# Second self attention: heads outside and batches inside, the next head projected beside attention, values in three split passes, division at the sum into x

## The chip, the cores and the metric

The kernel runs on one core of one Trainium2 chip. The metric is the device time of one execution, in microseconds (us), as the median of several runs; lower is better. The engines are TensorE (PE in the profile, with its weight loads as PEld), VectorE (DVE), ScalarE (ACT), GpSimd (POOL) and SyncE (SP), which here only issues DMAs. They run side by side and are held together by semaphores.

## What is computed

The reference is a decoder of two layers over x, 8 batches of 256 tokens with 256 channels. Six stages follow each other, each adding to x what it makes of the layer-normalised x. The change touches the fourth, the self attention of layer 1. Its reference, cut to what matters (HEADS = 8, DIM_HEAD = 128, context of 2 x 512 rows with 192 channels; `_split_heads` joins a head's batches, so that every query meets all 1024 keys):

```python
qh = _split_heads(jnp.einsum('bnq,qi->bni', x, Wq))
kh = _split_heads(jnp.einsum('bmc,ci->bmi', context, Wk))
vh = _split_heads(jnp.einsum('bmc,ci->bmi', context, Wv))
sim = jnp.einsum('hid,hjd->hij', qh, kh) * SCALE
mean = jnp.mean(sim, axis=-1, keepdims=True)
sim = (sim - mean) * ATTN_MATRIX_SCALE + mean
attn = jax.nn.softmax(sim, axis=-1)
out = jnp.einsum('hij,hjd->hid', attn, vh)
...
return jnp.einsum('bni,iq->bnq', out, Wout) + bout
```

So each of 8 heads has 2048 queries (8 batches of 256) and 1024 keys, 128 wide. The softmax doesn't see the subtraction of the mean, and the factor 1.5 goes into the scaling of the queries.

## The kernel before, in words

All arrays have 128 partitions. `x_all` holds x as 16 tiles of 128 tokens; `normalise` (L135) makes `xnT_all`, the normalised x with channels on partitions, for all batches, and issues the loads of the stage's weights on SP's queue. `psum` has 8 banks of 512 fp32 columns.

An fp32 matmul appears in the trace as two records of PE, each with its own weight load. Where more accuracy per pass is wanted, an operand is split: a high part in the faster fp32r format, made by ACT from PSUM, and a low part, the difference, made by DVE. `split_product` (L117) then makes three fp32r matmuls: high by high, low by high, high by low (L121 to L123).

`attention1` (L1366) works in two phases.

Keys and values come first, for all heads at once: 32 parts of 512 columns, 16 of keys and 16 of values. Each is two fp32 matmuls, one over the first 128 context channels and one over the other 64 (L1426 keys, L1429 values), into the eight banks in turn. ACT and DVE take the keys as high and low part (L1489, L1521); of the values one takes one half and the other the other half, as plain fp32 (L1489, L1525).

Then a loop over 8 batches (`Fori`, one body for all). SP copies the batch's slice of `xnT_all` to `xnT` (L1412). PE projects the queries of all 8 heads, fp32, 32 records (L1445); ACT and DVE take them as high and low (L1494, L1535). The attention itself runs over 16 units, a unit being one head and 128 tokens, in the order of `scores_softmax_value_order` (L877): scores of unit u, transposes of unit u-1, values of unit u-2.
- Scores: two halves of 512 keys, three fp32r passes each. DVE takes the negated row maximum (L1541), ACT the exponential with the row sum (L1501).
- Turn: 8 transposes of the 128x1024 weights to key-major form, through banks 4 and 5 (L1466). DVE copies one half out, ACT the other (L1548, L1508).
- Values: 8 fp32 matmuls of 128 columns, the turned weights stationary (L1475). DVE multiplies the result by the inverse of the sum into `o` (L1553, L1555).

When all 16 units of a batch are done, `turn_and_project` (L1334) transposes `o` in 16 transposes (L1341), ACT copies them (L1355), PE makes the output projection in 16 fp32 matmuls, 32 records (L1346), and DVE adds the result to x (L1569), to which it had added the bias at the start of the batch (L1532).

What sets the order: each engine runs its instructions strictly in the order written; there is no planner. PE has unit u's scores ahead of the transposes of u-1, so that the softmax of u runs beside them. The waits on PE at the batch's start are on `x_here`, `out_taken` and `q_taken` (L1436, L1438, L1441, L1452), at its end on `head_taken` (L1478) and the turned output (L1343).

Of the kernel before, what the change touches and what calls it, by code (L numbers as in the profile page):

```python
# [8 lines left out]
F32 = mybir.dt.float32  # L9
I32 = mybir.dt.int32  # L10
F32R = mybir.dt.float32r
# [4 lines left out]
P = 128  # L16
# [1317 lines left out]
def turn_and_project(pe, psum, ident, o, oT, w, turned, turned_taken, out_ready, b, chunks):  # L1334


    for t in range(TT):
        for g in range(chunks // 4):
            for i in range(4):
                lo = (4 * g + i) * P  # L1340
                ins = pe.transpose(psum[:, 2 * t + g, i * P:(i + 1) * P], o[:, t, lo:lo + P], ident[:])  # L1341
            ins.then_inc(turned, 1)
    pe.wait_ge(turned_taken, b * 4 + 4)  # L1343
    for t in range(TT):
        for k in range(chunks):
            ins = pe.matmul(psum[:, 4, t * D:(t + 1) * D], oT[:, t, k, :], w[:, k, :], start=(k == 0),  # L1346
                            stop=(k == chunks - 1))
    ins.then_inc(out_ready, 1)


def take_turned_output(act, psum, oT, turned, turned_taken, b):

    for n in range(4):
        act.wait_ge(turned, b * 4 + n + 1)
        act.activation(oT[:, n // 2, 4 * (n % 2):4 * (n % 2) + 4, :], psum[:, n, :].rearrange("p (k n) -> p k n", n=P),  # L1355
                       ACT.Copy).then_inc(turned_taken, 1)


# [4 lines left out]

def attention1(nc, norm, x_all, xnT_all, ident, psum, a):  # L1366
    with ExitStack() as stack:
# [6 lines left out]
        kT = [s.sb(f"kT_{part}", [P, AH, KEYS], F32R) for part in ("hi", "lo")]  # L1374
        qT = [s.sb(f"qT_{part}", [P, AH, T], F32R) for part in ("hi", "lo")]
        v = s.sb("v", [P, KB, AH * AD])
        xnT = s.sb("xnT", [P, CC, T])
        weights = [s.sb(f"weights{i}", [P, KEYS]) for i in range(2)]
        turned_w = s.sb("turned_w", [P, 2, KEYS])
        U = AH * TT  # L1380
        negmax, sums = s.sb("negmax", [P, U]), s.sb("sums", [P, U])

        o, oT = wk, turned_w[:].rearrange("p t (h d) -> p t h d", h=AH)
        loaded, x_here = s.sem("loaded"), s.sem("x_here")
        kv_ready, kv_act, kv_dve = s.sem("kv_ready"), s.sem("kv_act"), s.sem("kv_dve")
        q_ready, q_high, q_taken, scored, max_ready, exp_done, turned = (
            s.sem(n) for n in ("q_ready", "q_high", "q_taken", "scored", "max_ready", "exp_done", "turned"))
        half_taken = s.sems("half_taken", 2)
        summed, head_taken, own = s.sem("summed"), s.sem("head_taken"), s.sem("own")
        o_turned, o_turned_taken, out_ready, out_taken = (  # L1390
            s.sem(n) for n in ("o_turned", "o_turned_taken", "out_ready", "out_taken"))
        loads = []
        for dst, src in ((ctxT, a["ctxT"]), (wk, a["wk"]), (wv, a["wv"])):
# [4 lines left out]
        HALF = KEYS // 2  # L1398

        parts = [("k", h, half) for h in range(AH) for half in range(2)] + \  # L1400
                [("v", st, half) for st in range(KB) for half in range(2)]

        KP = 2 * AH

        act_did = lambda n: n + 1 if n < KP else KP + (n - KP) // 2 + 1
        dve_did = lambda n: n + 1 if n < KP else KP + (n - KP + 1) // 2

        @block.sync
        def _(sp):
            with sp.Fori(0, B) as b:  # L1410
                sp.wait_ge(q_ready, b * 4)
                sp.dma_start(xnT[:], xnT_all[:, bass.ds(b, 1), :, :]).then_inc(x_here, 16)  # L1412

        @block.tensor
        def _(pe):
            pe.wait_ge(loaded, 16 * len(loads))
            for n, (kind, i, half) in enumerate(parts):
                if n >= 8:

                    if n - 8 < KP or n % 2 == 1:  # L1420
                        pe.wait_ge(kv_dve, dve_did(n - 8))
                    else:
                        pe.wait_ge(kv_act, act_did(n - 8))
                for c, rows in enumerate((P, CTX - P)):
                    if kind == "k":
                        ins = pe.matmul(psum[:, n % 8, :], wk[0:rows, c, i * AD:(i + 1) * AD],  # L1426
                                        ctxT[0:rows, c, half * HALF:(half + 1) * HALF], start=(c == 0), stop=(c == 1))
                    else:
                        ins = pe.matmul(psum[:, n % 8, :], ctxT[0:rows, c, i * P:(i + 1) * P],  # L1429
                                        wv[0:rows, c, half * HALF:(half + 1) * HALF], start=(c == 0), stop=(c == 1))  # L1430
                ins.then_inc(kv_ready, 1)
            pe.wait_ge(kv_act, act_did(len(parts) - 1))
            pe.wait_ge(kv_dve, dve_did(len(parts) - 1))
            with pe.Fori(0, B) as b:
                S0 = b * U
                pe.wait_ge(x_here, b * 16 + 16)  # L1436

                pe.wait_ge(out_taken, b)  # L1438
                for m in range(AH // 2):
                    if m >= 2:  # L1440
                        pe.wait_ge(q_taken, b * 4 + m - 1)  # L1441
                    for j in range(2):
                        for c in range(CC):
                            lo = (2 * m + j) * AD
                            ins = pe.matmul(psum[:, 6 + m % 2, j * T:(j + 1) * T], wq[:, c, lo:lo + AD], xnT[:, c, :],  # L1445
                                            start=(c == 0), stop=(c == CC - 1))
                    ins.then_inc(q_ready, 1)
                for what, k in scores_softmax_value_order(U):
                    h, t = k // TT, k % TT
                    if what == "scores":  # L1450
                        if k == 0:
                            pe.wait_ge(q_taken, b * 4 + 4)  # L1452
                        if k >= 2:
                            pe.wait_ge(exp_done, S0 + k - 1)
                        for half in range(2):
                            ins = split_product(pe, psum[:, 2 * (k % 2) + half, :],
                                                [q[:, h, t * P:(t + 1) * P] for q in qT],
                                                [keys[:, h, half * HALF:(half + 1) * HALF] for keys in kT], True, True)
                        ins.then_inc(scored, 1)
                    elif what == "turn":  # L1460
                        pe.wait_ge(exp_done, S0 + k + 1)
                        for half in range(2):
                            pe.wait_ge(half_taken[half], S0 + k)
                            for j in range(4):
                                lo = half * HALF + j * P
# [3 lines left out]
                    else:  # L1469
                        for half in range(2):  # L1470
                            pe.wait_ge(half_taken[half], S0 + k + 1)
# [700 lines left out]
```

## Time and profile before

| | |
|---|---|
| median of 3 runs | 3400.91 us (3396.31 to 3406.21) |
| the profiled execution: time | 3403.3 us |
| the profiled execution: span of the trace | 3401.4 us |
| mean granted TensorE clock | 0.893 |
| PE busy | 2926.5 us, 86% of the span |
| weight loads (PEld) busy | 2085.1 us, 61% |
| DVE busy | 1863.0 us, 55% |
| ACT busy | 1617.8 us, 48% |
| POOL busy | 685.0 us, 20% |
| DMA | 60.88 MB, mean 18 GB/s |

The span runs from the first to the last instruction on the core; the time has 1.9 us around it. Shares of busy time are means over six stages with different limits; the stage of the change is the stretch from 1745 to 2571 us, between two runs of `normalise`. Matmuls are pipelined: the duration of one record is longer than the distance between the starts of two, and the distance is what PE's time is made of. The granted clock is 1.00 at 2.4 GHz and 0.50 at 1.2 GHz.

### The profile page before, as it was taken

Reading aid. Unit: us, or ns where it says so; the run is one execution under the profiler, and the core shown is the slowest. Engines: PE = TensorE matmul, PEld = TensorE weight load, DVE = VectorE, ACT = ScalarE, POOL = GpSimd, SP = SyncE. Lnnn points to the kernel's source line nnn. Section 1 sums busy time; section 2 is a strip of 40 time slices with the busy share of each in tenths; the row PEclk is TensorE's granted clock in tenths of the full one; section 3 lists DMA queues with packets and bytes.
Section 4 is the critical chain, followed back from the end, with each engine's and each line's share of the span. In section 5 each row is a group of like instructions: output and inputs, shape, how many; then the busy total and the mean of one; then the engine's idle time right before and its main releaser. Section 6 shows DMA issues by size and latency. Waiting matters only on the chain. (4 is left out here: it accounts for less than half of the span.)

```text
span 3401.4 us, 50572 instructions
## 1 busy us (share of the span) xinstructions
PE 2926.5 (86%) x17024; PEld 2085.1 (61%) x17024; DVE 1863.0 (55%) x4064; ACT 1617.8 (48%) x2895; POOL 685.0 (20%) x798
## 2 busy tenths in 40 slices
PE   6788888888655489999979999999998999968998
PEld 3344444444334356776732888888886777747887
DVE  4777877787633456656531444444444544544444
ACT  3887888878721234444511333333333555532221
POOL 1122222222100044444500000000001655620000
PEclk8888988899766689999965999999998999968999
DMA  2000000000010110110110000000002000010000
GB/s 94 4 4 3 3 0 3 3 3 0 1 35 19 54 44 23 23 42 22 21 58 0 4 3 3 3 3 3 3 0 85 4 6 6 3 69 22 6 6 28
DMA packets 88230, 60.88 MB, mean 18 GB/s; under 512 B 54816, under 2 KB 76704, under 8 KB 87648
## 3 DMA queue, kind: packets, MB, share of 16 engines
q1 hardware_dynamic: 88160, 59.99, 5.8%
q8 instruction: 39, 0.64, 0.1%
q14 instruction: 31, 0.25, 0.0%
HBM read 41.10 MB, written 8.39 MB: 15 GB/s over the span
## 5 line engine op out<-in xcount | busy, mean ns | idle before, releaser
L1772 POOL TENSOR_SCALAR x_weights<-x_weights,x_sums 128x256 f32<-128x256 f32 x256 | 231.7, 924 | 1066.5 <-DVE x_sums L1809 1066.5
L670 DVE SCALAR_TENSOR_TENSOR a_w<-a_w,a_sinks 128x384 f32<-128x384 f32 x512 | 332.7, 714 | 31.5 <-ACT a_w L505 31.5
L1074 POOL TENSOR_SCALAR f_weights<-f_weights,f_sums 128x256 f32<-128x256 f32 x256 | 232.2, 924 | 271.2 <-DVE f_sums L1304 271.2
L1501 ACT ACTIVATE a_weights<-psum,a_negmax 128x1024 f32<-128x1024 f32 x128 | 142.5, 1114 | 293.1 <-DVE a_negmax L1541 293.1
L484 ACT ACTIVATE a_e<-psum 128x1024 f32<-128x1024 f32 x192 | 195.4, 1018 | 158.0 <-PE psum L343 118.9
L1475 PE MATMUL psum<-a_v,a_turned_w 128*128 128x128 f32 x2048 | 248.3, 275 | 0.0
L1475 PEld LDWEIGHTS psum<-a_v,a_turned_w 128*128 128x128 f32 x2048 | 238.1, 192 | 0.0
L1541 DVE TENSOR_REDUCE a_negmax<-psum 128x1 f32<-128x1024 f32 x128 | 156.7, 1224 | 124.9 <-PE psum L123 124.0
L1232 ACT ACTIVATE f_weights<-psum,f_negmax 128x256 f32<-128x256 f32 x256 | 117.8, 472 | 215.1 <-DVE f_negmax L1298 215.1
L340 PE MATMUL psum<-a_qT,a_kT_half 32*128 32x512 f32 x512 | 166.5, 730 | 60.6 <-DVE a_w L685 48.7
L685 DVE SCALAR_TENSOR_TENSOR a_w<-a_e,psum 128x512 f32<-128x512 f32 x256 | 162.6, 675 | 96.1 <-ACT a_e L486 86.6
L486 ACT ACTIVATE a_e<-a_e 128x1024 f32<-128x1024 f32 x192 | 202.9, 1057 | 6.1
L1742 ACT ACTIVATE x_weights<-x_masked_s,x_negmax 128x256 f32<-128x256 f32 x256 | 126.9, 496 | 147.1 <-DVE x_negmax L1805 147.0
L505 ACT ACTIVATE a_w<-a_w 128x1536 f32<-128x1536 f32 x128 | 179.4, 1472 | 0.4
L1466 PE MATMUL psum<-all_ident,a_weights 128*128 128x128 f32 x1024 | 133.8, 274 | 9.5 <-ACT a_weights L1501 9.5
L1466 PEld LDWEIGHTS psum<-all_ident,a_weights 128*128 128x128 f32 x1024 | 118.3, 140 | 29.9 <-ACT a_weights L1501 14.2
L370 PE MATMUL psum<-a_w,a_v 128*32 128x512 f32 (+1 forms) x1024 | 114.6, 575 | 19.8 <-DVE a_w L670 19.8
L188 PE MATMUL psum<-all_ident,ln_xn 128*128 128x128 f32 x192 | 53.4, 434 | 82.3 <-DVE ln_xn L177 82.3
L121 PE MATMUL psum<-a_kT_hi,a_qT_hi 128*128 128x512 f32 x256 | 110.7, 432 | 11.3 <-DVE a_qT_lo L1535 11.3
L340 PEld LDWEIGHTS psum<-a_qT,a_kT_half 32*128 32x128 f32 x512 | 44.1, 210 | 113.5 <-DVE a_w L685 59.8
L343 PEld LDWEIGHTS psum<-a_future,a_ident_r 128*128 128x128 f32 x256 | 42.5, 209 | 113.5 <-issue 113.5
L566 POOL TENSOR_TENSOR a_ctxn<-a_ctx,a_vnull 128x256 f32<-128x256 f32 x64 | 45.1, 725 | 330.2 <-DVE a_ctx L640 330.2
(304 smaller groups left out, 6820.1 us busy)
## 6 DMA issues: line engine op xcount, KB each, us to landing
a_xnT<-all_xnT_all SPq DMA_DIRECT2D x16, 256.0 KB, 2.3
x_ctxT<-in_x_ctxT SPq DMA_DIRECT2D x16, 256.0 KB, 2.7
f_xnT<-all_xnT_all SPq DMA_DIRECT2D x16, 256.0 KB, 2.3
f_pv_rows<-f_pv SPq DMA_DIRECT2D x8, 512.0 KB, 3.1
f_pv_groups<-f_pv_rows SPq DMA_DIRECT2D x8, 512.0 KB
f_w<-in_f_w SPq DMA_DIRECT2D x2, 2048.0 KB, 10.3
all_x_all<-in_x SPq DMA_DIRECT2D x1, 2048.0 KB, 8.4
a_wq<-in_a_wq SPq DMA_DIRECT2D x2, 1024.0 KB, 9.2
```

What stands on the lines that cost most here:

```text
L340: pe.matmul(psum[:, 2 * x + h, :], kT_half[rows[h], step % 2, g, 0:P], qT[rows[h], g, 2 * x:2 * x + 2, :], start=True, stop=False)
L484: act.activation(e[:, x, :], psS[x], ACT.Exp).then_inc(exp_done, 1)
L486: act.activation(e[:, x, :], e[:, x, :], ACT.Ln, bias=1.0).then_inc(ln_done, 1)
L505: act.activation(wu, wu, ACT.Silu, scale=SILU_SCALE).then_inc(silu_done, 1)
L670: ins = dve.scalar_tensor_tensor(part, part, sinks[:, col:col + 1], part, ALU.is_ge, ALU.mult)
L685: ins = dve.scalar_tensor_tensor(wu[:, h, 2 * x:2 * x + 2, 0:T], by_branch(e[:, x, :]), CAP, by_branch(psS[x]), ALU.min, ALU.max)
L1074: ins = pool.tensor_scalar(w, w, sums[:, k, h, t:t + 1], None, ALU.mult)
L1466: ins = pe.transpose(psum[:, 4 + half, j * P:(j + 1) * P], weights[k % 2][:, lo:lo + P], ident[:])
L1475: ins = pe.matmul(psum[:, 6 + k % 2, 0:AD], turned_w[:, k % 2, j * P:(j + 1) * P], v[:, j, h * AD:(h + 1) * AD], start=(j == 0), stop=(j = ...
L1501: act.activation(weights[k % 2][:], psum[:, 2 * (k % 2):2 * (k % 2) + 2, :].rearrange("p a n -> p (a n)"), ACT.Exp, bias=negmax[:, k:k + 1 ...
L1541: dve.tensor_reduce(negmax[:, k:k + 1], psum[:, 2 * (k % 2):2 * (k % 2) + 2, :].rearrange("p a n -> p (a n)"), AX.X, ALU.max, negate=True) ...
L1772: ins = pool.tensor_scalar(w, w, sums[:, k, h, t:t + 1], None, ALU.mult)
```

## The change

The order of the loops is turned round: 8 heads outside, 8 batches inside, written out as 64 pairs (head, batch) without a hardware loop. Keys, values and queries are held for two heads only, and all three as high and low part; those of the first head are made in 8 steps ahead of the pairs, and pair n makes one eighth of the keys or values (`project_kv`, a quarter of the keys or two blocks of the values) and one batch's queries (`project_q`) for the next head. Scores and transposes of a unit stay as they were. The turned weights are now split too, by ACT (high) and DVE (low), for all halves of both units of a pair; the value product is 8 blocks of three fp32r passes with the values stationary and 256 tokens moving, so that its result already has channels on partitions. It isn't divided: ACT copies it to `oT`, PE projects it with the head's part of the output weights (two fp32 matmuls of 256 columns), and DVE multiplies by the inverse sums in adding to x, once per pair and head. POOL adds the bias to x at the start. The copies of `xnT_all` on SP, the transposes of `o` and `turn_and_project` are gone. The diff, cut to its core:

```diff
-            with pe.Fori(0, B) as b:
...
-                        for j in range(KB):
-                            ins = pe.matmul(psum[:, 6 + k % 2, 0:AD], turned_w[:, k % 2, j * P:(j + 1) * P],
-                                            v[:, j, h * AD:(h + 1) * AD], start=(j == 0), stop=(j == KB - 1))
...
-                turn_and_project(pe, psum, ident, o, oT, wo, o_turned, o_turned_taken, out_ready, b, AH)
+            def project_kv(n):
+                h, i = n // B, n % B
+                if n >= B:
+                    wait(pe, out_taken, n - B - 1)
+                    wait(pe, kv_low, n)
+                elif n >= 4:
+                    pe.wait_ge(kv_low, n - 3)
+                if n == B:
+                    pe.wait_ge(q_low, B)
+                for j in range(1 if i < 4 else 2):
+                    for c, rows in enumerate((P, CTX - P)):
+                        if i < 4:
+                            ins = pe.matmul(kv_bank(n), wk[0:rows, c, h * AD:(h + 1) * AD],
+                                            ctxT[0:rows, c, i * QUARTER:(i + 1) * QUARTER], start=(c == 0), stop=(c == 1))
+                        else:
+                            lo = (2 * (i - 4) + j) * P
+                            ins = pe.matmul(kv_bank(n)[:, j * AD:(j + 1) * AD], ctxT[0:rows, c, lo:lo + P],
+                                            wv[0:rows, c, h * AD:(h + 1) * AD], start=(c == 0), stop=(c == 1))
+                ins.then_inc(kv_made, 1)
...
+            def turn(u):
+                pe.wait_ge(exp_done, u + 1)
+                for half in range(2):
+                    wait(pe, low_taken, 2 * (u - 1) + half + 1)
...
+            def values(n):
+                h = n // B
+                pe.wait_ge(low_taken, 4 * n + 4)
+                pe.wait_ge(q_low, min(n + 2 + B, A1_PAIRS))
+                wait(pe, oT_ready, n)
+                for j in range(KB):
+                    ins = split_product(pe, psum[:, 6, 0:T], [z[:, h % 2, j, :] for z in v],
+                                        [z[:, n % 2, j, :] for z in turned_w], j == 0, j == KB - 1)
+                ins.then_inc(summed, 1)
+
+            def out(n):
+                h = n // B
+                pe.wait_ge(oT_ready, n + 1)
+                pe.wait_ge(kv_low, min(n + 2 + B, A1_PAIRS))
+                wait(pe, out_taken, n)
+                for t in range(TT):
+                    ins = pe.matmul(psum[:, 7, t * D:(t + 1) * D], oT[:, t * P:(t + 1) * P], wo[:, h, :], start=True, stop=True)
+                ins.then_inc(out_made, 1)
...
+            for n in range(B):
+                project_kv(n)
+                project_q(n)
+            for n in range(A1_PAIRS + 2):
+                here = n < A1_PAIRS
+                if here:
+                    scores(2 * n)
+                if 1 <= n <= A1_PAIRS:
+                    turn(2 * n - 1)
+                if n >= 2:
+                    out(n - 2)
+                if n + B < A1_PAIRS:
+                    project_q(n + B)
+                if here:
+                    scores(2 * n + 1)
+                    turn(2 * n)
+                if 1 <= n <= A1_PAIRS:
+                    values(n - 1)
+                if n + B < A1_PAIRS:
+                    project_kv(n + B)
```

The orders for a pair on ACT (first), the bias on POOL (second), and the order on DVE (third):

```diff
+            for n in range(A1_PAIRS + 1):
+                here = n < A1_PAIRS
+                if n >= 1:
+                    for half in range(2):
+                        high(2 * n - 1, half)
+                if here:
+                    exps(2 * n)
+                if n + B < A1_PAIRS:
+                    q_hi(n + B)
+                if here:
+                    for half in range(2):
+                        high(2 * n, half)
+                    exps(2 * n + 1)
+                if n >= 1:
+                    take_oT(n - 1)
+                if n + B < A1_PAIRS:
+                    kv_hi(n + B)
...
+            for b in range(B):
+                x_b = x_all[:, b * TT:(b + 1) * TT, :]
+                pool.tensor_tensor(x_b, x_b, bo[:].unsqueeze(1).to_broadcast([P, TT, D]), ALU.add).then_inc(x_biased, 1)
...
+            for n in range(A1_PAIRS + 2):
+                here = n < A1_PAIRS
+                if here:
+                    row_max(2 * n)
+                if 1 <= n <= A1_PAIRS:
+                    for half in range(2):
+                        low(2 * n - 1, half)
+                    invert(2 * n - 1)
+                if n >= 2:
+                    add_out(n - 2)
+                if n + B < A1_PAIRS:
+                    q_lo(n + B)
+                if here:
+                    row_max(2 * n + 1)
+                    for half in range(2):
+                        low(2 * n, half)
+                    invert(2 * n)
+                if n + B < A1_PAIRS:
+                    kv_lo(n + B)
```

`high` and `low` are 128x512 from a bank of turned weights, `add_out` is two operations of 128x256, `kv_hi`, `kv_lo`, `q_hi`, `q_lo` and `take_oT` are 128x256.

## Rows read from the trace of the kernel before

**Rows 1.** The page's first line.
```profile
span 3401.4 us, 50572 instructions
```

**Rows 2.** Busy by stretch: us, PE, PEld, DVE, ACT, POOL, PEclk, DMA share, GB/s.
```profile
1745.00:1874.00 129.00, 128.25 (x128) 31.96 (x128) 16.56 (x24) 15.61 (x25) 0.00 (x0) 0.50 0.01 2
1874.00:1878.00 4.00, 3.51 (x8) 2.86 (x9) 0.72 (x2) 0.00 (x0) 0.00 (x0) 0.50 0.01 2
1880.00:1884.00 4.00, 3.83 (x18) 3.00 (x16) 1.39 (x2) 1.33 (x3) 0.00 (x0) 1.00 0.00 0
...
1974.00:2060.00 86.00, 81.16 (x559) 73.06 (x558) 39.79 (x70) 32.91 (x57) 0.00 (x0) 1.00 0.01 3
1745.00:2571.00 826.00, 785.02 (x4608) 622.34 (x4608) 339.00 (x588) 278.51 (x481) 0.00 (x0) 0.92 0.01 3
```

**Rows 3.** Who waited for whom in 1745 to 2571: us in total, times, longest.
```profile
ACT a_weights L1501 <- DVE a_negmax L1541: 293.1, 128, 3.7
...
PE psum L1466 <- ACT a_weights L1501: 9.5, 8, 1.2
```

**Rows 4.** Timeline of one unit: start us, us, engine, line, operation, xcount.
```profile
2001.25 0.48 PE L121 MATMUL psum<-a_kT_hi,a_qT_hi 128*128 128x512 f32 x1
...
2001.57 0.39 PE L122 MATMUL psum<-a_kT_lo,a_qT_hi 128*128 128x512 f32 x1
...
2002.73 1.03 PE L1466 MATMUL psum<-all_ident,a_weights 128*128 128x128 f32 x8
2002.93 1.22 DVE L1541 TENSOR_REDUCE a_negmax<-psum 128x1 f32<-128x1024 f32 x1 [0.97 <-PE psum L123]
...
2003.60 1.95 PE L1475 MATMUL psum<-a_v,a_turned_w 128*128 128x128 f32 x16
...
2004.27 1.11 ACT L1501 ACTIVATE a_weights<-psum,a_negmax 128x1024 f32<-128x1024 f32 x1 [2.36 <-DVE a_negmax L1541]
...
2005.31 0.48 PE L121 MATMUL psum<-a_kT_hi,a_qT_hi 128*128 128x512 f32 x1
```

**Rows 5.** Timeline of the key projection, weight loads of two fp32 matmuls.
```profile
1749.03 0.50 PEld L1426 LDWEIGHTS psum<-a_ctxT,a_wk 128*128 128x128 f32 x2 [1.50 <-issue]
...
1751.03 0.50 PEld L1426 LDWEIGHTS psum<-a_ctxT,a_wk 64*128 64x128 f32 x2 [1.50 <-issue]
```

**Rows 6.** Timeline: output projection and query projection of one batch.
```profile
2041.94 7.17 PE L1346 MATMUL psum<-a_wo,a_turned_w 128*128 128x256 f32 x32 [0.84 <-ACT a_turned_w L1355]
...
2049.99 7.14 PE L1445 MATMUL psum<-a_xnT,a_wq 128*128 128x256 f32 x32 [0.88 <-DVE all_x_all L1569]
```

**Rows 7.** Timeline of the experts' stage: passes of split products, the first and the seventh.
```profile
3077.41 0.28 PE L123 MATMUL psum<-f_xnT_hi,f_w_in_lo 128*128 128x256 f32 x1
...
3078.12 0.28 PE L123 MATMUL psum<-f_xnT_hi,f_w_in_lo 128*128 128x256 f32 x1
```

**Rows 8.** Timeline of the switch attention: 64-row matmuls, transposes, the next group.
```profile
1693.86 1.14 PE L1171 MATMUL psum<-f_kT,f_qT 64*128 64x256 f32 x8
1694.93 1.09 PE L1185 MATMUL psum<-all_ident,f_weights 128*128 128x128 f32 x8
1695.95 1.08 PE L1199 MATMUL psum<-f_turned_w,f_v 128*64 128x256 f32 x8
```

**Rows 9.** Groups of instructions in 1745 to 2571, DVE and ACT.
```profile
L1521 DVE TENSOR_TENSOR a_kT_lo<-psum,a_kT_hi 128x512 fp32r<-128x512 f32 x16 | 11.1, 691 | 56.1 <-ACT a_kT_hi L1489 56.1
...
L1508 ACT ACTIVATE a_turned_w<-psum 128x512 f32<-128x512 f32 x128 | 75.3, 588 | 6.0 <-PE psum L1466 6.0
```

**Rows 10.** Busy time by stretch, first self attention (columns as in rows 2).
```profile
97.00:107.00 10.00, 10.00 (x32) 3.11 (x32) 6.90 (x10) 4.76 (x5) 0.00 (x0) 0.50 0.01 2
...
110.90:117.00 6.10, 6.10 (x30) 2.82 (x26) 4.43 (x8) 5.85 (x5) 0.00 (x0) 1.00 0.00 0
```

**Rows 11.** DMA queues and busy time (columns as in rows 2) of 2614 to 2700.
```profile
q8 instruction: 4, 0.07, 0.3%
...
2614.00:2700.00 86.00, 83.53 (x550) 61.54 (x552) 42.55 (x175) 48.92 (x143) 52.82 (x59) 0.98 0.03 7
```

More of the change, by code:

```diff
@@ L1331, in _ @@
             over_batches(dve, body)
[L1334 to L1356, printed above, removed]
 AH, AD = 8, 128
@@ L1397, in attention1, with kv_bank, q_bank @@
         block = stack.enter_context(nc.Block())
[L1398 to L1412, printed above, removed]
+        def kv_bank(n):
+            return psum[:, 2 * n % 8, 0:T] if n < B else psum[:, 7, 0:T]
+        def q_bank(n):
+            return psum[:, (2 * n + 1) % 8, 0:T] if n < B else psum[:, 6, T:2 * T]
         @block.tensor
@@ L1416, in _ @@
             pe.wait_ge(loaded, 16 * len(loads))
[L1417 to L1431, printed above, removed]
@@ L1481, in part_of @@
-        def part_of(to, n):
-            kind, i, half = parts[n]
-            return to[:, i, half * HALF:(half + 1) * HALF]
+            def project_kv(n):
[17 more added lines that the diff above has]
+                ins.then_inc(kv_made, 1)
@@ new lines, in project_q @@
+            def project_q(n):
+                h, b = n // B, n % B
+                if n >= B:
+                    pe.wait_ge(kv_low, B)
+                    pe.wait_ge(q_low, n)
+                    wait(pe, oT_ready, n - B - 1)
+                elif n >= 4:
+                    pe.wait_ge(q_low, n - 3)
+                for c in range(CC):
+                    ins = pe.matmul(q_bank(n), wq[:, c, h * AD:(h + 1) * AD], xnT_all[:, b, c, :],
+                                    start=(c == 0), stop=(c == CC - 1))
+                ins.then_inc(q_made, 1)
@@ new lines, in turn @@
+            def turn(u):
+                pe.wait_ge(exp_done, u + 1)
+                for half in range(2):
+                    wait(pe, low_taken, 2 * (u - 1) + half + 1)
+                    for j in range(4):
+                        lo = (4 * half + j) * P
+                        ins = pe.transpose(psum[:, 4 + half, j * P:(j + 1) * P], weights[u % 2][:, lo:lo + P], ident[:])
+                    ins.then_inc(turned, 1)
+            def values(n):
[7 more added lines that the diff above has]
+                ins.then_inc(summed, 1)
@@ new lines, in exps, with take_oT @@
+            def exps(u):
+                act.wait_ge(max_ready, u + 1)
+                wait(act, turned, 2 * (u - 1))
+                wait(act, inverted, u - STAT_RING + 1)
+                act.activation(weights[u % 2][:], psum[:, 2 * (u % 2):2 * (u % 2) + 2, :].rearrange("p a n -> p (a n)"),
+                               ACT.Exp, bias=negmax[:, u % STAT_RING:u % STAT_RING + 1],
+                               accum_out=sums[:, u % STAT_RING:u % STAT_RING + 1]).then_inc(exp_done, 1)
+            def take_oT(n):
+                act.wait_ge(summed, n + 1)
+                wait(act, out_made, n)
+                act.activation(oT[:], psum[:, 6, 0:T], ACT.Copy).then_inc(oT_ready, 1)
```

221 lines of the change are left out of this document (90 added, 131 removed).

## Prediction

> **What bounds the kernel now.** I read the page, then busy time by stretch, the stage's waits, and last the timeline of one unit. The profiled execution has a span of 3401.4 us and a time of 3403.3 [rows 1]; the median of the three runs, 3400.9, is 2.4 lower, so the sum is made against 3403.3 and then moved by -2.4. The second self attention lies at 1745 to 2571, 826 us; PE is busy 785 of them, DVE 339, ACT 279 [rows 2]. The reader should see three pieces in it. First, all keys and values are projected in 129 us, in which PE is always busy and the granted clock is 0.50 (1.2 GHz) throughout. Then the clock goes to 1.00 (2.4 GHz) within some 4 us of the query projection. Then come eight batches of 86 us at 1.00 [rows 2].
>
> In a batch PE sets the pace. ACT waits 293 us for DVE's row maximum, but PE waits for the exponentials only 9.5 us in the whole stage, in 8 places [rows 3]: ACT's wait is idle time of an engine that isn't the bound. One unit (head, half of the tokens) shows it: from one first score matmul to the next 2001.25 to 2005.31 = 4.06 us, without a hole on PE. Within it: six score passes, 0.32 for the first and then (2002.73 - 2001.57)/5 = 0.232 each, 1.48 together; eight transposes 0.87 (0.109 each); sixteen records of eight fp32 value matmuls 1.71 (0.107 each) [rows 4]. The first pass after fp32 work costs 0.09 more than the others: call it a change of kind, 0.1. A batch is 16 such units, 65 us; the other 21 are four waits between phases, 7.1 us of query projection and 7.2 of output projection (32 records each, (7.14 - 0.38)/31 = 0.218 per record of 256 columns) [rows 6], and 2 of output transposes.
>
> **The change, part by part.** What counts is PE's time for a pair (head, batch), 64 pairs.
> - Scores, twice: 12 x 0.232 = 2.78. Weight transposes, 16 x 0.109 = 1.74. Both stay.
> - Values: fp32 becomes three fp32r passes, with the value tile stationary and 256 tokens moving: 8 blocks x 3 = 24 passes in place of 32 records. The experts' stage runs just this form, 128x128 against 128x256, fp32r, at (3078.12 - 3077.41)/6 = 0.118 [rows 7]: 24 x 0.118 = 2.83 instead of 3.42. Saves 0.6.
> - Changes of kind: three per pair (two scores, values), 0.3; two before. Bounds 0 and 0.1 each.
> - Output projection per pair: 2 matmuls, 4 records x 0.218 = 0.87, as before. The transposes of the normalised output (0.22 per pair) and the four waits per batch go.
> - Sum without projections: 2.78 + 1.74 + 2.83 + 0.30 + 0.87 = 8.52; x 64 = 545.
> - Queries of the next head, in 56 pairs: 4 records, 0.87. Keys or values of the next head, in 56 pairs: the same columns as before, now in the warm loop. A key part is 4 records of 256 (0.87), a value part 8 of 128 (8 x 0.107 = 0.86).
> - Change of row count: these parts alternate a 128-row and a 64-row chunk. Before, each fp32 matmul took 2.00 us there (loads at 1749.03 and 1751.03) [rows 5], where 1024 columns at 1.2 GHz are 1.71: 0.29 for each change. In the switch attention at full clock, eight transposes that follow 64-row matmuls take 1.02 (1694.93 to 1695.95) [rows 8] against 0.87: 0.15. I take 0.15, since it was measured at the loop's clock and is half of 0.29; ends 0 and 0.29. A key part has two changes, a value part four, mean 3: 0.45. Projections: 0.87 + 0.87 + 0.45 = 2.19; x 56 = 123.
> - Ahead of the loop: first head's keys, values and queries for all batches, 8 steps. At full clock 0.87 + 0.87 and the changes, 17.6 in all; at half clock 4 x (2.29 + 1.74) + 4 x (2.86 + 1.74) = 34.5. Keys and values alone never raised the clock in 129 us, queries did in some 4 us [rows 2], and in the first attention 10 us of full PE work stayed at 0.50 before it rose by 110.9, 14 us after its start [rows 10]. The new stretch is half the one and half the other: I take the rise at 14 us, 14 + 20.5/2 = 24; ends 18 and 35.
> - Start and end: the first query's rest (about 1.2), the first transpose waiting for its exponential (0.4), and behind the last scores the lower half of the weights (0.9), the copy to oT (0.8), the add (1.1): 4.4. Handovers as in rows 4: PE to DVE 0.2, DVE to ACT 0.12.
>
> Sum: 545 + 123 + 24 + 4.4 + 1.2 of stage change = 698, against 826: -128. 3403.3 - 128 = 3275, and with -2.4, **3273**.
>
> **What must stay hidden.** DVE per pair: two maxima 2.44 [rows 4], four lower halves 2.76 [rows 9], and four operations half as wide as those of 0.69, so at most 2.76: 8.0, and two reciprocals of one column. ACT: two exponentials 2.6 with their sums, four copies 2.36 [rows 9], three narrower ones under 1.8: 6.7. Both lie under PE's 10.7, but their queues are in order. The tightest place is the transpose of the even unit: row maximum, then ACT's two upper halves of the odd unit before, then the exponential, done 2.9 us after the scores' end; PE has 0.87 + 0.87 + 0.87 + 1.48 = 4.1 of other work there. Slack 1.2, and 0.3 in the last eight pairs, where there is no projection. Values wait for the query's lower half of the same pair (DVE done near 5.7 of the pair, values due at 6.4). Output waits for the key part's lower half, done 1.3 before it is due. Costed at nothing: eight 256 KB copies and their SP queue (no wait of the stage names them); ACT's eight table loads (ACT waits anyway); the bias on POOL, which starts at once, while the first add comes after two pairs and then one add per 10.7 us (at DVE's 0.69 each, 6 us; uncovered it would cost those 6).
>
> The new stage is written out for 64 pairs, without loops. PE takes some 140 instructions per pair. The cross attention's written-out stretch at 2614 to 2700 fetched 4 instruction blocks in 86 us while PE was hardly stopped [rows 11]; I take zero.
>
> **Against the trace, a rule that speaks against the change.** The experts' rows show loads of the same 128 rows hidden under 256-column passes: 0.118 per pass, hardly above 256 columns at 2.4 GHz [rows 7]. The Trainium skill, TensorE: Matmul & The Clock Gate, section Part 3: Packing small matmuls, says that a weight load overlaps a running matmul only when the row groups differ. By that rule all 24 loads of a pair's values would be exposed; this trace disagrees with it, so the sum goes by the rows. It is the first rival below.
>
> **Rivals.**
> 1. Exposed loads in the values (ends slower). Each pass would carry its load: by half of the K/V matmul's 0.29 [rows 5], 0.15 x 24 x 64 = +223, 3496. It decides from 128/1536 = 0.083 per pass. For: three loads per block where values had two. Against: the same form at 0.118. Chance 0.03.
> 2. The softmax chain stalls PE. If handovers or the order of ACT's queue eat the slack of 1.2 and 1 us more in each pair, +64: 3337. For: slack is only 0.3 in the last eight pairs. Against: the schedule above. Chance 0.10; still faster.
> 3. The cold clock comes along: 64-row parts keep the clock at 0.50 in the prologue and at times in the loop. Prologue +11; each 10 us of loop at half clock +5. With six such dips 3315. Against: batches stayed at 1.00 in spite of their waits. Chance 0.07.
> 4. More gain: no cost for changes of rows (-25) and of kind (-13): 3235. Chance 0.08.
> 5. The change doesn't do what it says for the values: at 0.142 per pass, 24 passes cost the old 3.42. +38, 3311. For: passes that alternate between two kinds of operand tiles; against: the experts' do the same [rows 7]. Chance 0.03.
>
> **How the numbers follow.** The forecast keeps 0.69, its own span 3245 to 3310. Range: from the free changes (3235) to rival 2 less some (3330). Faster by over 0.3% (about 10 us, what this measurement can tell): all but rival 1 and unforeseen stalls, 0.95; within 0.3%, 0.01; slower 0.04, rival 1 and its like.
>
> **What the profile would show.** PE busy without holes, a pair every 10.6 to 10.8 us (8.5 in the last eight); clock 1.00 from the loop's start; value passes 0.118 apart; no 129 us stretch at 0.50; stage near 698 us. Wrong, if PE shows idle before the transposes (waiting for ACT), or value passes 0.2 apart, or a clock of 0.50 within the loop.

## The result, and the profile after

The changed kernel takes **3268.7 us** (median of four runs, 3266.4 to 3270.6), against 3399.3 for the kernel before (four runs): a ratio of 0.961, 95% interval 0.9596 to 0.9624, 130.7 us less. The forecast was 3273, with a range of 3235 to 3330. The profiled execution took 3266.4 us.

The page of the profile after: the span, the engines' busy time, the instruction queue, and the groups of the value passes, of the two parts that the turned weights now have, and of the row maximum.

```profile
span 3264.6 us, 49578 instructions
...
PE 2818.9 (86%) x16640; PEld 2049.9 (63%) x16640; DVE 1942.7 (60%) x4248; ACT 1693.0 (52%) x3120; POOL 694.7 (21%) x806
...
q8 instruction: 68, 1.11, 0.1%
...
L1506 ACT ACTIVATE a_turned_w_hi<-psum 128x512 fp32r<-128x512 f32 x256 | 139.0, 595 | 195.2 <-PE psum L1440 195.1
...
L1570 DVE TENSOR_REDUCE a_negmax<-psum 128x1 f32<-128x1024 f32 x128 | 156.7, 1224 | 89.8 <-PE psum L123 89.8
...
L1577 DVE TENSOR_TENSOR a_turned_w_lo<-psum,a_turned_w_hi 128x512 fp32r<-128x512 f32 x256 | 163.7, 681 | 2.3 <-ACT a_turned_w_hi L1506 2.3
L121 PE MATMUL psum<-a_turned_w_hi,a_v_hi 128*128 128x256 f32 x512 | 150.2, 293 | 0.7 <-DVE a_turned_w_lo L1577 0.7
```

Against [rows 1] the span is 136.8 us shorter. PE has 108 us less to do, DVE 80 more and ACT 75 more, and neither of the two became the bound: the lower halves of the turned weights (681 ns) cost about what the row of the old key halves had promised (691) [rows 9].

Busy time by stretch, with the columns of [rows 2]: the two halves of the part ahead of the pairs, the middle of the pairs, and the whole stage from its first projection to its last add.

```profile
1744.80:1758.90 14.10, 14.09 (x28) 8.02 (x28) 2.55 (x6) 2.30 (x6) 9.81 (x8) 0.50 0.00 0
1758.90:1770.30 11.40, 11.40 (x53) 8.46 (x52) 3.82 (x9) 3.46 (x9) 0.00 (x0) 1.00 0.01 2
1777.50:2390.00 612.50, 605.65 (x3782) 526.30 (x3782) 375.00 (x690) 316.44 (x633) 0.00 (x0) 1.00 0.00 1
1744.80:2441.40 696.60, 686.31 (x4224) 591.73 (x4224) 416.89 (x768) 353.03 (x705) 9.81 (x8) 0.99 0.00 1
```

The stage takes 696.6 us where it took 824.8 (1745.05 to 2569.85), **128.2 less**. The 129 us at a granted clock of 0.50 [rows 2] are gone; 14 us of it are left at the start, and within the pairs the clock is 1.00 throughout, with PE busy 98.9% of the time. Of the 136.8 us of the span, 8.3 lie behind the stage, in code that the change leaves alone: from the last add of this stage to the end of the span, 823.2 us against 831.5, at a mean granted clock of 0.94 against 0.93. In another run below (E2), with the same code there, the stretch takes 833.8 us at 0.93, so this is not put down to the change.

The waits of the stage, to be held against [rows 3]:

```profile
ACT a_turned_w_hi L1506 <- PE psum L1440: 195.1, 127, 2.7
...
PE psum L121 <- issue: 6.8, 7, 1.0
...
PE psum L121 <- DVE a_qT_lo L1565: 1.0, 1, 1.0
...
PE psum L121 <- DVE a_turned_w_lo L1577: 0.7, 1, 0.7
...
PE psum L1461 <- ACT a_oT L1523: 0.5, 1, 0.5
...
PE psum L1440 <- ACT a_weights L1515: 0.3, 1, 0.3
```

ACT now waits for PE, and no longer 293 us for DVE. Of PE's own waits, all but one line come once, at the start or the end of the stage, 2.5 us together. The line with seven times 1.0 us (`issue` means that the profile names nobody that PE waited for) was not foreseen.

A pair (head, batch) on the timeline (columns as in [rows 4]), from one first score pass to the next; where rows are left out, they are the other passes of the same product.

```profile
2001.11 0.50 PE L121 MATMUL psum<-a_kT_hi,a_qT_hi 128*128 128x512 f32 x1
...
2002.60 1.04 PE L1440 MATMUL psum<-all_ident,a_weights 128*128 128x128 f32 x8
...
2003.47 1.03 PE L1461 MATMUL psum<-a_wo,a_oT 128*128 128x256 f32 x4
...
2004.34 1.03 PE L1413 MATMUL psum<-all_xnT_all,a_wq 128*128 128x256 f32 x4
...
2005.01 0.59 PE L121 MATMUL psum<-a_kT_hi,a_qT_hi 128*128 128x512 f32 x1
...
2006.59 1.03 PE L1440 MATMUL psum<-all_ident,a_weights 128*128 128x128 f32 x8
...
2007.38 0.36 PE L121 MATMUL psum<-a_turned_w_hi,a_v_hi 128*128 128x256 f32 x1
...
2007.70 0.28 PE L123 MATMUL psum<-a_turned_w_hi,a_v_lo 128*128 128x256 f32 x1
...
2010.22 0.28 PE L123 MATMUL psum<-a_turned_w_hi,a_v_lo 128*128 128x256 f32 x1
...
2010.34 1.63 PE L1399 MATMUL psum<-a_wv,a_ctxT 128*128 128x128 f32 x8
...
2011.91 0.50 PE L121 MATMUL psum<-a_kT_hi,a_qT_hi 128*128 128x512 f32 x1
```

From start to start, in us: scores 1.49, transposes 0.87, output 0.87, queries 0.67, scores 1.58, transposes 0.79, values 2.96, value part 1.57; together 10.80 us. The value passes stand (2010.22 - 2007.70)/21 = 0.120 apart. A pair with a key part takes 10.41, one of the last eight 8.26.

The start of a new head, on PE's timeline:

```profile
1849.87 1.32 PE L1399 MATMUL psum<-a_wv,a_ctxT 64*128 64x128 f32 x6
1852.17 0.47 PE L121 MATMUL psum<-a_kT_hi,a_qT_hi 128*128 128x512 f32 x1 [0.97 <-issue]
```

Here PE stands still for 0.97 us. The first scores of a head wait for `kv_low` at (h + 1) * B (L1422), which counts the values' parts too, and the last of these has just left PE; ACT and DVE must still take it. Scores need only the keys. Seven changes of head, seven such waits.

**Where the 128 us came from.** Values took 3.42 in two units before [rows 4] and take 2.96 now, 64 times: 29. Keys and values took 128 us from the first record to the last; now 28 x (1.15 + 1.57) = 76 in the pairs and 15 ahead of them: 37. The third part are waits between phases and the transposes of the output. PE's waits in the stage of the kernel before, and the output transposes of one batch:

```profile
PE psum L121 <- DVE a_qT_lo L1535: 11.3, 8, 1.4
...
PE psum L1346 <- ACT a_turned_w L1355: 6.8, 8, 0.8
PE psum L1445 <- DVE all_x_all L1569: 6.1, 7, 0.9
PE psum L1341 <- DVE a_wk L1555: 4.1, 8, 0.5
...
2039.13 1.97 PE L1341 MATMUL psum<-all_ident,a_wk 128*128 128x128 f32 x16 [0.52 <-DVE a_wk L1555]
```

With the 9.5 of [rows 3] and a single wait of 1.2 the waits make 39, and 8 x 1.97 of transposes 16: 55. The three parts make 121 of the 128; the other 7 are the net of smaller terms, the seven new waits (-7) among them. The experiments ask whether each part stands alone.

### The profile page after: what moved, and what is told of

It reads as the page before. It is cut to its first block and busy times, and to the rows that moved or that the text cites. A ratio compares the mean times of both kernels' runs of the same rounds, so it can differ in the third digit from the quotient of the medians.

```text
span 3264.6 us, 49578 instructions
## 1 busy us (share of the span) xinstructions
PE 2818.9 (86%) x16640; PEld 2049.9 (63%) x16640; DVE 1942.7 (60%) x4248; ACT 1693.0 (52%) x3120; POOL 694.7 (21%) x806
## 5 line engine op out<-in xcount | busy, mean ns | idle before, releaser
L1506 ACT ACTIVATE a_turned_w_hi<-psum 128x512 fp32r<-128x512 f32 x256 | 139.0, 595 | 195.2 <-PE psum L1440 195.1
L1577 DVE TENSOR_TENSOR a_turned_w_lo<-psum,a_turned_w_hi 128x512 fp32r<-128x512 f32 x256 | 163.7, 681 | 2.3 <-ACT a_turned_w_hi L1506 2.3
L121 PE MATMUL psum<-a_turned_w_hi,a_v_hi 128*128 128x256 f32 x512 | 150.2, 293 | 0.7 <-DVE a_turned_w_lo L1577 0.7
L123 PE MATMUL psum<-a_turned_w_hi,a_v_lo 128*128 128x256 f32 x512 | 144.9, 283 | 0.0
L122 PE MATMUL psum<-a_turned_w_lo,a_v_hi 128*128 128x256 f32 x512 | 144.8, 283 | 0.0
L121 PE MATMUL psum<-a_kT_hi,a_qT_hi 128*128 128x512 f32 x256 | 118.9, 464 | 7.9 <-issue 6.8
## 6 DMA issues: line engine op xcount, KB each, us to landing
f_w<-in_f_w SPq DMA_DIRECT2D x2, 2048.0 KB, 10.1
```

What stands on the lines that cost most here:

```text
L121: pe.matmul(out, lhsT[0], rhs[0], start=start, stop=False)
L122: pe.matmul(out, lhsT[0], rhs[1], start=False, stop=False)
L123: return pe.matmul(out, lhsT[1], rhs[0], start=False, stop=stop)
L1577: dve.tensor_tensor(lo, psum[:, 4 + half, :].rearrange("p (j t) -> p j t", t=P), hi.bitcast(F32), ALU.subtract)\
```

## The experiments

Stage means the stretch from the first projection of this attention to its last add, 696.6 us in the changed kernel. E1 to E5, E7 and E8 are edits of the changed kernel, B1 to B3 of the kernel before; each ratio is to the kernel before, run on the same chip beside it.

**E1: values unsplit in the new form.**

```diff
-                    ins = split_product(pe, psum[:, 6, 0:T], [z[:, h % 2, j, :] for z in v],
-                                        [z[:, n % 2, j, :] for z in turned_w], j == 0, j == KB - 1)
+                    ins = pe.matmul(psum[:, 6, 0:T], v[0][:, h % 2, j, :], turned_w[0][:, n % 2, j, :],
+                                    start=(j == 0), stop=(j == KB - 1))
```

(The high parts of `v` and `turned_w` are then plain fp32; their two lines are left out here.)

> The changed kernel with the value product in fp32 again (the high tiles hold full fp32, one fp32 matmul of 256 columns per block, two records each); ACT's and DVE's copies stay, so only PE's passes change. Theory (PE sets the pace of every pair): 16 records x 0.218 = 3.49 us against the 2.96 that the value stretch took in the changed kernel, +0.53 per pair x 64 = +34, about 3303. Rival (the softmax chain sets the pace): within 10 us of 3269.

Measured: 3309.9 us, ratio 0.9738 (0.9713 to 0.9762); stage 733.3, +36.7. On PE's timeline the sixteen fp32 records take 3.46 us:

```profile
1997.84 3.62 PE L1450 MATMUL psum<-a_turned_w_hi,a_v_hi 128*128 128x256 f32 x16
2001.30 1.63 PE L1399 MATMUL psum<-a_wv,a_ctxT 128*128 128x128 f32 x8
```

Every pair from the third on is 0.55 to 0.60 longer, and 64 of them make the 37. So the split passes are worth that much in this order, and the 24 loads are hidden: with three passes per block in place of two records PE is still faster.

**E2: the second block of a value part begins with its 64-row chunk**, so that a part changes its row count twice and not four times.

```diff
-                    for c, rows in enumerate((P, CTX - P)):
+                    for c, rows in ((0, P), (1, CTX - P)) if j == 0 else ((1, CTX - P), (0, P)):
...
-                                            wv[0:rows, c, h * AD:(h + 1) * AD], start=(c == 0), stop=(c == 1))
+                                            wv[0:rows, c, h * AD:(h + 1) * AD], start=(c == j), stop=(c != j))
```

> In the value parts the second block takes its 64-row chunk first, so that the row count goes 128, 64, 64, 128: two changes in place of four, same matmuls. Theory (a change of row count costs PE about 0.15 to 0.18): a value part falls from 1.57 us to about 1.25, 32 of them, -9 to -11, about 3259. Rival (fp32 matmuls of 128 columns are slow by themselves): value parts stay at 1.57, 3269.

Measured: 3267.3 us, ratio 0.9613 (0.9594 to 0.9632): the median doesn't show it. The stage does, 689.0, -7.6:

```profile
2004.59 1.44 PE L1399 MATMUL psum<-a_wv,a_ctxT 128*128 128x128 f32 x8
2005.79 0.47 PE L121 MATMUL psum<-a_kT_hi,a_qT_hi 128*128 128x512 f32 x1
```

A value part takes 1.20 instead of 1.57, **0.18 per change of row count**, and its pair 10.41 instead of 10.80; 28 of them are -10.6. The waits at a new head grew from 1.0 to 1.2 (+1.3), and the clock rose later ahead of the pairs (+1.8). Behind the stage this execution took 833.8 us, 10.6 more than that of the changed kernel, at a mean granted clock of 0.93 instead of 0.94: in the profiled execution this is what covers the gain in the total. On the total alone the run is inconclusive.

**E3: the second chunk padded with zeros to 128 rows**; no changes of row count, and twice the rows in these matmuls.

```diff
+                for pad in pads:
+                    pool.memset(pad, 0.0)
...
+                  [z[CTX - P:P, 1, :] for z in (ctxT, wk, wv)])
...
-                    for c, rows in enumerate((P, CTX - P)):
+                    for c, rows in enumerate((P, P)):
```

> The second context chunk is padded with zeros to 128 rows (POOL clears the pads during the layer norm), so that keys and values have no change of row count at all; same number of matmuls and columns. Theory: key parts fall from 1.16 to 0.87 us, value parts from 1.57 to 0.86, 28 of each in the loop, -28, and 3 to 10 more ahead of the loop, about 3235. Rival (the columns cost it, not the rows): 3269; if the extra rows cost something, slower.

Measured: 3224.9 us, ratio 0.9505 (0.948 to 0.9529); stage 655.5, **-41**, a little more than expected.

```profile
1740.85 2.05 PE L1402 MATMUL psum<-a_ctxT,a_wk 128*128 128x256 f32 x4 [0.82 <-PEq L137]
...
1744.40 1.38 PE L1402 MATMUL psum<-a_ctxT,a_wk 128*128 128x256 f32 x4
...
2006.15 1.03 PE L1402 MATMUL psum<-a_ctxT,a_wk 128*128 128x256 f32 x4
2006.83 0.58 PE L121 MATMUL psum<-a_kT_hi,a_qT_hi 128*128 128x512 f32 x1
```

A key part takes 0.68 instead of 1.15, a value part 0.81 instead of 1.57, and the pairs 10.0 to 10.1 instead of 10.41 and 10.80. The clock rises 4.2 us after the stage's start, not 14.1, and the first transposes start 21.5 us after it, not 30.7. Rows of zeros cost PE no time here; the changes cost it 33 us in the pairs and 9 ahead of them, the later rise of the clock included.

**E4: queries of the first head ahead of its keys and values** (the same on ACT and DVE).

```diff
             for n in range(B):
-                project_kv(n)
                 project_q(n)
+            for n in range(B):
+                project_kv(n)
```

> Ahead of the loop, all eight query parts first, then the eight key and value parts, on all three engines. Theory (key and value parts hold the clock at 1.2 GHz, query parts let it rise within 5 us as before the change): the stretch takes 19 to 20 us in place of 25.4, -6, about 3263. Rival (the rise comes some 14 us after the start whatever is run): 25 us, 3269.

Measured: 3263.7 us, ratio 0.96 (0.9584 to 0.9616), which by itself could not be told from the changed kernel's; stage 691.1, -5.5. Busy time by stretch of its start:

```profile
1746.80:1750.00 3.20, 3.20 (x9) 2.62 (x10) 0.42 (x1) 0.38 (x1) 3.12 (x3) 0.56 0.00 0
1750.00:1754.00 4.00, 4.00 (x20) 3.54 (x19) 1.70 (x4) 1.90 (x5) 4.00 (x4) 1.00 0.00 0
1754.00:1767.00 13.00, 12.81 (x55) 8.00 (x53) 4.24 (x10) 3.62 (x11) 2.72 (x3) 1.00 0.01 2
```

With matmuls of 128 rows first the clock rises 2.8 us after the start, and the keys and values behind them, with their changes of row count, don't lose it again: this part takes 20.0 us in place of 25.4.

**E5: the row maximum computed twice**, to find how much room DVE has.

```diff
+                dve.tensor_reduce(spare[:, u:u + 1], psum[:, 2 * (u % 2):2 * (u % 2) + 2, :].rearrange("p a n -> p (a n)"),
+                                  AX.X, ALU.max, negate=True)
```

> The changed kernel with every row maximum computed twice on DVE, the first into a spare column: 1.22 us more in the softmax chain of each unit, and DVE at about 9.7 us of each pair's 10.7. Theory (slack of 1.2 us before the even unit's transposes in 56 pairs, 0.3 in the last eight): 0 to 0.2 per pair in the 56, about 1 in each of the eight, +8 to +20, 3277 to 3289. Rival (the chain is already at its limit): +1.2 to 2.4 per pair, +77 or more.

Measured: 3299.0 us, ratio 0.9702 (0.9678 to 0.9726), 30 more than the changed kernel where 8 to 20 were expected; stage 722.4, +25.8, and far from the rival's 77. On the timeline:

```profile
2004.98 1.04 PE L1441 MATMUL psum<-all_ident,a_weights 128*128 128x128 f32 x8
2005.51 0.41 DVE L1566 SCALAR_TENSOR_TENSOR a_qT_lo<-psum,a_qT_hi 128x256 fp32r<-128x256 f32 x1
...
2006.02 0.35 PE L121 MATMUL psum<-a_turned_w_hi,a_v_hi 128*128 128x256 f32 x1
```

The values start 1.04 behind the transposes, not 0.79, since they wait for the query's lower half, done at 2005.92: the pairs take 10.64 and 11.04, +0.24 each, 13 in 56. In every such pair but the first (0.17) the values start 0.10 after that lower half is done; in the changed kernel it is 0.98. In the last eight pairs the transposes wait 0.56 for the exponential, and a pair takes 9.04 instead of 8.26: 6 more. The first two pairs take 3 more, and the clock rose later ahead of the pairs, +3.3. So the tightest place in the pairs with projections is not the one that I had called so (transposes, slack 1.2) but the values behind `q_low`: done at 2006.39 and due at 2007.38 in the changed kernel, a slack of 1.0, which the second maximum's 1.2 just uses up. In the last eight it is the transposes.

**B1: the kernel before, with E3's padding.**

```diff
...
-                for c, rows in enumerate((P, CTX - P)):
+                for c, rows in enumerate((P, P)):
```

(The lines that clear the pads are as in E3.)

> The kernel before the change with the second context chunk padded with zeros to 128 rows, nothing else. Theory A (the alternation of 128 and 64 rows held the clock at 1.2 GHz in its 129 us of keys and values): the clock rises within 4 to 14 us, 128 records x 0.436 = 56 us at full clock, the stretch takes 58 to 63, -66 to -71, about 3330. Rival B (the stream of 512-column fp32 matmuls keeps the clock low by itself): only the 64 changes of 0.29 go, -19, about 3381.

Measured: 3320.6 us, ratio 0.9769 (0.9743 to 0.9794), 85 us under the kernel before. Busy time by stretch of its key and value projection:

```profile
1740.00:1743.00 3.00, 2.62 (x3) 1.17 (x4) 0.00 (x0) 0.07 (x1) 0.00 (x0) 0.50 0.23 87
1743.00:1746.00 3.00, 3.00 (x7) 1.33 (x6) 0.69 (x1) 0.60 (x1) 0.00 (x0) 0.76 0.00 0
1746.00:1798.00 52.00, 51.57 (x121) 22.52 (x119) 15.62 (x23) 15.01 (x24) 0.00 (x0) 1.00 0.00 0
```

The phase at 0.50 [rows 2], 128.3 us from its first record to its last (1745.05 to 1873.30), takes 57.2 (1740.38 to 1797.57), with the clock at 1.00 from 4.1 us after its start: **71 us from padding alone**. Outside it, in the two profiled executions, 2.2 us lie in the first batch behind it, which finds the clock at 1.00 already, 4.7 ahead of the stage and 5.1 behind it, where the code is the same. While the clock is still at 0.50, this run also shows what the same columns take without a change of row count, by the loads of two records, that is one fp32 matmul:

```profile
1742.22 0.33 PEld L1433 LDWEIGHTS psum<-a_ctxT,a_wk 128*128 128x128 f32 x1 [0.52 <-issue]
...
1743.93 0.33 PEld L1433 LDWEIGHTS psum<-a_ctxT,a_wk 128*128 128x128 f32 x1 [0.52 <-issue]
```

1.71 us, against 2.00 [rows 5]: the 0.29 per change is measured here. B1 leaves two theories: the changes of row count kept the clock down, or the idle rows of the 64-row matmuls did. B2 and B3 part them.

**B2: the kernel before, with chunks of 96 and 96 rows** (no changes, and a quarter of the rows idle all the time, as many as before on average; the loads of the context and the weights are cut to match).

```diff
...
-                for c, rows in enumerate((P, CTX - P)):
+                for c, rows in enumerate((CTX // 2, CTX // 2)):
```

> The kernel before with the context split into two chunks of 96 rows in place of 128 and 64; no change of row count, a quarter of the rows idle as before. Theory A1 (holes): as with full rows, about 3321. Theory A2 (idle rows): the clock stays at 1.2 GHz, -19, about 3382.

**B3: the kernel before, with four parts' 128-row matmuls and then their four of 64 rows** (the same matmuls; one change of row count where there were four).

```diff
-            for n, (kind, i, half) in enumerate(parts):
+            for n, c in [(4 * g + m, c) for g in range(len(parts) // 4) for c in range(2) for m in range(4)]:
...
```

> The kernel before with its key and value projection in groups of four parts: four 128-row chunks, then four 64-row chunks, same matmuls and rows, 16 changes of row count in place of 64. Theory A1 (the holes at the changes held the clock down): the clock rises soon, 129 us become 55.8 + 16 x 0.3 + the slow start, 60 to 67, about 3335. Theory A2 (rows left idle held it down): the clock stays at 1.2 GHz, 48 changes x 0.29 go, -14, about 3387.

Measured: B2 3324.8 us, ratio 0.9783 (0.9764 to 0.9802); B3 3327.2 us, ratio 0.9788 (0.9767 to 0.9809). Busy time by stretch in B2, where the phase starts at 1744.40:

```profile
1743.00:1746.00 3.00, 2.18 (x5) 1.02 (x5) 0.00 (x0) 0.77 (x2) 0.00 (x0) 0.50 0.07 25
1746.00:1798.00 52.00, 52.00 (x117) 22.76 (x116) 15.19 (x22) 13.69 (x23) 0.00 (x0) 0.96 0.01 4
```

And in B3, where it starts at 1743.53 (second row: the first query projection, just behind the phase):

```profile
1746.00:1798.00 52.00, 52.00 (x114) 20.46 (x113) 15.23 (x22) 13.13 (x22) 0.00 (x0) 0.99 0.00 0
...
1805.40:1808.80 3.40, 3.40 (x10) 2.71 (x9) 0.30 (x1) 0.60 (x1) 0.00 (x0) 0.50 0.00 0
```

Both are at 0.96 and more in the long stretch, and the phase takes 58 us in B2 and 60 in B3, where it took 128. Idle rows are not the cause: B2 has as many and B3 the very same matmuls. It is the alternation of row counts, matmul by matmul, with the 0.29 us that each change costs. Whether the clock stays down for the time lost at the changes or for the changes themselves, and why, is not shown, only that it rises when they are gone or four times fewer. B3 also shows the clock falling to 0.50 once more, for 3.4 us, behind its phase with 16 changes and a wait of 1.2 us on PE. B1 and B2, without changes and with the same wait, show no such fall; one execution of each does not tell whether the changes have to do with it.

**E7: scores wait for the keys alone**, and the first values of a head for its values.

```diff
                 if b == 0:
-                    pe.wait_ge(kv_low, (h + 1) * B)
+                    pe.wait_ge(kv_low, h * B + 4)
...
                 pe.wait_ge(low_taken, 4 * n + 4)
+                if n % B == 0:
+                    pe.wait_ge(kv_low, (h + 1) * B)
```

> The changed kernel, but the first scores of a head wait only for its keys (parts 0 to 3), and its first values for the value parts. Theory: the seven waits of 1.0 us at the change of head (6.8 us in the trace, named issue) come from the last value part being made just ahead of them; they go, about 3262. Rival (something else, such as instruction fetch): they stay, 3269.

Measured: 3259.8 us, ratio 0.9583 (0.9564 to 0.9602), an interval that overlaps the changed kernel's; the reading rests on the trace. All of PE's waits on the passes of L121 in its stage:

```profile
PE psum L121 <- DVE a_qT_lo L1567: 1.0, 1, 1.0
...
PE psum L121 <- DVE a_turned_w_lo L1579: 0.7, 1, 0.7
```

The seven waits are gone and none has taken their place: a pair at a new head takes 10.78 like its neighbours, not 11.83. The stage is 691.3, 5.3 shorter, as the clock rose later ahead of the pairs this time (+1.8).

**E8: E3 and E7 together.**

> The changed kernel with both: full rows and waiting for the keys alone. The gains add: 3225 - 7 = 3218. It should be the fastest kernel of the study.

Measured: **3222.5 us**, ratio 0.948 (0.9462 to 0.9497), the fastest kernel of the study, 179 us under the kernel before and 46 under the changed one; stage 647 us. The intervals of E3 and E8 overlap; that E7's part adds to E3's rests on the stage, 8.3 us shorter than E3's, and on the pairs at a new head, 10.01 us where E3's take 11.23. The 3218 that were expected lie at the lower end of its runs (3218.0 to 3224.8).

## Why the prediction was right

**The bound.** That PE sets the pace, before and after, held in every step. ACT and DVE took 155 us more work in the whole kernel and held PE up for 9.3 us in the stage, 2.5 at its start and end and 6.8 at the changes of head. The argument from ACT's 293 us of waiting (idle time of an engine that isn't the bound) was right.

**The sum.** 698 us were forecast for the stage and 696.6 measured. Term by term:
- Scores and values with their changes of kind: 5.91 forecast, 1.49 + 1.58 + 2.96 = 6.03 measured. The passes are 0.120 apart (0.118), but the first value pass takes 0.20.
- Transposes 1.74 forecast, 1.66 measured; output 0.87 and 0.87. Queries 0.87 forecast, 0.67 measured: the scores behind them start 0.20 earlier than four records take, and the 0.09 that they then take longer is in the 1.58 above.
- Key part 1.17 forecast, 1.15 measured; value part 1.46 forecast, 1.57 measured. Between the ends of 0 and 0.29 for a change of row count, 0.15 was taken from the row at the loop's clock [rows 8]; E2 shows 0.18. A small error of size.
- A pair: 10.71 forecast on average, 10.60 measured without the heads' changes; the last eight 8.52 forecast, 8.26 measured. Together 8 us too much. Most of it lies in the changes of kind, for which 0.3 per pair were taken: a pair without its key or value part takes 9.23, and its passes and records at the measured distances make 12 x 0.232 + 16 x 0.109 + 24 x 0.120 + 8 x 0.218 = 9.15, so they cost 0.08.
- **Missed**: the wait at a new head, 7 x 1.0. The prediction listed who waits for the lower halves of queries and keys, and asked of the values' parts only that the next pairs' output waits for them; L1422, where the scores do, was not gone through. E7 shows its price.
- Ahead of the pairs: 24 forecast, 25.4 measured, with the clock rising 14.1 us after the start as taken. That this came so near has luck in it: with much the same work ahead of it the rise came 18.0 us after the start in E7, 21.2 in E5 and 21.4 in E2, and 14.3 in E1.

So 8 us too much stand against 8 missing (7 and 1.4), and the sum is nearer than its terms; either alone would have left it well within the range.

**Slips in the working.** None moves the forecast itself. The columns of a key matmul take 1.71 us at 0.50, as B1 shows, but not because 1024 columns run at 1.2 GHz, which would be 0.85: an fp32 record of 256 columns takes 0.218 at 1.00 [rows 6], and the matmul is two records of 512 at half that clock. In the first rival 0.15 x 24 x 64 is 230; the 223 go with 0.145. In the fourth, free changes of kind would give 19 by the sum's own term (64 x 0.30), not 13, and the lower end of the range would be 3229. And the tightest place was named as the transposes, with a slack of 1.2, though the prediction's own times gave the values behind the query's lower half less (5.7 against 6.4); E5 shows that it is there, with 1.0 in the changed kernel.

**The rivals.** The first, exposed loads in the values (+223), is refuted: 0.120 per pass and E1's +37 for taking the passes away. The page that it went by, the Trainium skill, TensorE: Matmul & The Clock Gate, says in its Part 3 that a load overlaps only where row groups differ; what this case shows is the opposite, loads hidden where the row count stays (0.120 per pass) and time lost where it changes (0.18). The second, stalls by the softmax chain, did not come; E5 shows how near it was, since 1.2 us more on DVE per unit cost 26 us in the stage, 3.3 of them by the later clock. The third, the cold clock in the pairs, did not come either: 1.00 throughout. Of the fourth, free changes of row count are refuted by E2 and E3, while nearly free changes of kind are what the timeline shows (0.08 per pair). The fifth is refuted by 0.120 per pass, 2.96 per pair where 3.42 was, and by E1: fp32 in their place is 0.55 to 0.60 slower per pair.

**What was right for a reason that I had only half seen.** I took the 129 us at 0.50 as given for keys and values, and their move beside the queries as a gain of the new order. B1 to B3 show that the gain was to be had without the new order: the alternation of 128 and 64 rows was the cause, and 71 of the 128 us went with it. So of the change's 131 us, its own are the waits between phases with the output's transposes (55) and the values (29); the 37 of the keys and values are about half of the 71 that padding gives there, and E3, with both, takes the other part: another 41 us from the stage of the changed kernel. With padding on both sides the change is still worth some 96 us (B1 to E3: stage 751.6 to 655.5, medians 3320.6 to 3224.9, not measured side by side).

## What to carry to other kernels

When one phase runs at half the granted clock though PE is shown busy all the time, look at the weight loads' shapes before moving the phase: here two row counts in turn cost 71 of 128 us, and padding with zeros, equal chunks, or grouping equal row counts gave back 71, 70 and 68 of them. An order that interleaves the next head's projections with attention pays by closing the waits between phases; then go through every wait that counts a producer of two things (here keys and values on one semaphore), since at a head's change it waits for the later of them. A second pass on an engine with apparent slack is a cheap test of how much slack there is, and shows which wait is next.

## What the runs showed of the hardware that I had not expected

- PE's records hide the holes: in [rows 2] PE is 99% busy over 129 us at a clock of 0.50, with loads 2.00 us apart [rows 5] where the columns take 1.71 (B1). The same columns, padded, run at 1.00 from 4.1 us after the start (B1).
- Once at 1.00, the clock stayed there in spite of such changes in the pairs (two or four each) and behind E4's queries. In these runs the changes kept it from rising; that they never bring it down is not shown, since it fell for 3.4 us behind B3's 16.
- Padding a 64-row matmul to 128 rows cost no PE time at all: a key part went from 1.15 to 0.68 (E3).
- The written-out stage fetches its code without holding PE up: 68 packets on the instruction queue for 39 before, 29 more; none of PE's waits names it, and the only ones without a name, at the changes of head, went with E7.
- Two executions of the same untouched stages differed by 10 us (823 and 834), with a mean granted clock of 0.94 in the one and 0.93 in the other; an effect of that size is read from the stage, not from the total.
